# Sixteen-head attention in a four-layer kernel: head pairs in two halves of the partitions, parts staged through a DRAM scratch

## The reference

```python
# layer 0; layer 2 is the same without biases, and causal
q = (x @ Wq.T + bq).reshape(b, s, 16, 8)
k = (x @ Wk.T + bk).reshape(b, s, 16, 8)
v = (x @ Wv.T + bv).reshape(b, s, 16, 8)
w = jnp.einsum('bshd,bzhd->bhsz', q, k) / jnp.sqrt(8.0)
w = jax.nn.softmax(w, axis=-1)
vw = jnp.einsum('bhsz,bzhd->bshd', w, v).reshape(b, s, 128)
x = _layernorm(x + vw @ Wo.T + bo)
```

## Time and profile before

| | |
|---|---|
| median of 3 runs | 1496.15 us (1493.22 to 1500.85) |
| the profiled execution | 1497.72 us |
| its span in the profile | 1496.0 us |
| TensorE (PE) matmul busy | 1135.4 us (76%) |
| VectorE (DVE) busy | 952.6 us (64%) |
| ScalarE (ACT) busy | 614.8 us (41%) |
| GpSimd (POOL) busy | 486.2 us (32%) |
| mean granted TensorE clock | 0.846 of full speed |
| bytes moved by DMA | 117.02 MB, 152567 packets |

### The profile page before, as it was taken

One profiled execution on the slowest core, in us unless ns is written; L12 is line 12 of the kernel. 1 busy time (PEld: TensorE's weight loads), 2 busy tenths in 40 slices (PEclk: granted clock), 3 DMA queues, 4 the chain that ended last, 5 costly groups with the idle time before them and its releaser, 6 DMA issues.

```text
span 1496.0 us, 32177 instructions
## 1 busy us (share of the span) xinstructions
PE 1135.4 (76%) x9171; PEld 822.8 (55%) x9171; DVE 952.6 (64%) x3478; ACT 614.8 (41%) x1352; POOL 486.2 (32%) x695
## 2 busy tenths in 40 slices
PE   2799899889199994776728998999976899337950
PEld 1355555554188883664516776777654566225730
DVE  3688888886423324996836776777557687761237
ACT  1266556656044441335403554555554232113410
POOL 6112433434535453233441111111024111352553
PEclk9599889989599996997657999999977797558985
DMA  4655445531367767211025443444010000133523
GB/s 118 72 59 62 70 67 76 69 59 40 115 196 201 207 198 228 74 43 32 18 31 70 53 53 48 52 55 47 17 29 28 22 25 11 44 110 92 167 78 91
DMA packets 152567, 117.02 MB, mean 78 GB/s; under 512 B 16001, under 2 KB 140674, under 8 KB 152322
## 3 DMA queue, kind: packets, MB, share of 16 engines
q1 hardware_dynamic: 145282, 101.18, 34.2%
q0 software_dynamic: 7168, 14.37, 2.9%
HBM read 47.26 MB, written 23.41 MB: 47 GB/s over the span
## 4 chain that ended last, share of the span: by engine, by line
PE 46%; DVE 23%; issue 10%; DMA 7%; POOL 6%; SPq 3%; ACT 3%; DVEq 1%; POOLq 0%; ACTq 0%
PE po L1485 7%; PE po L431 6%; DVE xg L334 4%; PE pt L1479 4%; DVE mx L601 4%; PE pm L1479 3%; SPq L367 3%; PE pt L391 2%; PE pt L394 2%; PE pm L412 2%; DMA xs<-xg 2%; POOL rstd L327 2%; PE pm L417 2%; PE pm L418 2%; PE p L522 2%
## 5 line engine op out<-in xcount | busy, mean ns | idle before, releaser
L601 DVE TENSOR_REDUCE mx<-pm 128x2 f32<-128x512 f32 (+1 forms) x512 | 306.3, 619 | 163.2 <-PE pm L418 97.8
L553 ACT ACTIVATE ex<-pt 128x512 f32<-128x512 f32 (+1 forms) x512 | 271.1, 544 | 207.9 <-PE pt L391 99.3
L324 POOL TENSOR_SCALAR ve<-mv 128x2 f32<-128x2 f32 x96 | 25.5, 266 | 560.6 <-DVE mv L318 560.6
L1562 POOL DMA_INDIRECT result<-ye,to_row x128 | 122.9, 960 | 151.3 <-issue 107.2
L431 PE MATMUL po<-ex,va 128*32 128x256 f32 (+1 forms) x2048 | 157.7, 381 | 5.2 <-ACT ob L562 5.2
L412 PE MATMUL pm<-ks,qs 96*128 96x256 bf16 x512 | 110.7, 303 | 11.5 <-DVE mx L601 10.9
L308 ACT COPY xt<-p 128x256 f32<-128x256 f32 x112 | 41.8, 373 | 175.1 <-PE p L304 175.1
L1485 PE MATMUL po<-he,we 128*128 128x256 f32 (+1 forms) x448 | 112.9, 395 | 0.6 <-DVE yt L1523 0.4
L334 DVE TENSOR_SCALAR xg<-res,mv,rstd 128x128 f32<-128x128 f32 (+1 forms) x192 | 90.1, 536 | 32.6 <-POOL rstd L327 32.6
L391 PE MATMUL pt<-qs,ks 99*128 99x256 bf16 x512 | 105.7, 292 | 6.4 <-DMA qs<-mt 3.1
L303 PE MATMUL p<-ident,xs 128*128 128x128 f32 x112 | 40.4, 361 | 85.2 <-DMA xs<-xg 81.9
(11 more groups left out here) (281 smaller groups left out, 2788.5 us busy)
## 6 DMA issues: line engine op xcount, KB each, us to landing
we<-in_pack SPq DMA_DIRECT2D x40, 514.5 KB
xs<-xg SPq DMA_DIRECT2D x112, 128.0 KB, 2.2
qs<-parts SPq DMA_DIRECT2D x192, 64.0 KB
ks<-parts SPq DMA_DIRECT2D x192, 64.0 KB
we<-in_pack SPq DMA_DIRECT2D x16, 512.0 KB
xe<-sorted SPq DMA_DIRECT2D x56, 132.0 KB, 2.2
yr<-result SPq DMA_DIRECT2D x48, 128.0 KB, 2.2
xr<-xg SPq DMA_DIRECT2D x32, 128.0 KB, 4.8
```

Of the source, the lines that this page charges most:

```text
L553: nc.scalar.activation(ex[j % 2][:, 2 * u:2 * u + 2, lo:S], pt[:, u, :].rearrange("p (b k) -> p b k", k=S)[:, :, lo:S], ACT.Exp).then_inc( ...
L601: nc.vector.tensor_reduce(mx[q.slot % 2][:, qt, 4 * b + 2 * u:4 * b + 2 * u + 2], pm[:, u, :].rearrange("p (b k) -> p b k", k=S)[:, :, 0:h ...
L1562: pool.indirect_dma_start(out=rows, out_offset=bass.IndirectOffsetOnAxis(ap=to_row[q.slot][0:m, i:i + 1], axis=0), in_=ye[q.slot][0:m, i, ...
```

## The change

Heads 2h and 2h+1 form a pair. The even head of each pair sits in partitions 0 to 47 of the stacks and the odd one in partitions 64 to 111; the maxima follow in rows 48 to 50 and 112 to 114. Each stack is now 128 partitions by 8 pairs by 256 tokens. For every (j, u) one function `scores` issues what `scores_m` and `scores_t` issued, alternating between the two: for u = 0 `scores_m` works on the even heads and `scores_t` on the odd ones, for u = 1 the other way round, so that two neighbouring matmuls read different halves of the partitions and write different PSUM banks. All waits of both are ahead of the first matmul. The causal mask also fits in 64 rows: an identity half times a mask half, twice (256 and 128 columns, each for both heads), in place of two products of 128 columns.

Parts go to the stacks in two hops: six DMAs write them (in the order of the six products) to a DRAM scratch `scr`, SP waits until all six have landed, and four DMAs of 48 partitions read them back, one per stack and half. The zeroing of the stacks on POOL and its semaphore are gone; DVE sets rows 32 to 63 and 96 to 127 of `ks` to one at the start. Two transposes of 48 rows replace one of 96 for the maxima; `mt` is 48 by 256. POOL makes the mask and identity halves with 12 affine selects where it made two.

```diff
-        STACK, MAX_AT = 48, 96
-        ks = [sb(f"ks{i}", [MAX_AT + 3, HEADS, S], BF16) for i in range(SLOTS)]
+        STACK, HALF, HP = 48, P // 2, HEADS // 2
+        ks = [sb(f"ks{i}", [P, HP, S], BF16) for i in range(SLOTS)]
...
+        scr = nc.dram_tensor("scr", (SLOTS, 2, PRODUCTS, P, S), BF16).ap()
...
-                    for t in range(2):
-                        sp.dma_start(qs[q.slot][MAX_AT:MAX_AT + 3, :, t * P:t * P + P],
-                                     mt[q.slot % 2][STACK * t:STACK * t + STACK, :]).then_inc(mrows[q.slot], 16)
+                    for of_pair in range(2):
+                        r = HALF * of_pair + STACK
+                        sp.dma_start(qs[q.slot][r:r + 3, :, :],
+                                     mt[q.slot % 2][3 * HP * of_pair:3 * HP * (of_pair + 1), :]).then_inc(mrows[q.slot], 16)
                 if (q := at(1)):
                     wait_apart(sp, parts_pool, 2 * (a + q.n + 1), passed)
+                    if a == 0:
+                        sp.wait_ge(consts_v, CONSTS_V)
+
+                    s = q.slot % 2
+                    for c, n_c in ((0, 3), (3, 2), (5, 1)):
+                        sp.dma_start(scr[q.slot, 0, c:c + n_c].rearrange("c p k -> p c k"), parts[s][:, 0:n_c, 0, :]
+                                     ).then_inc(to_scr, 16)
+                        sp.dma_start(scr[q.slot, 1, c:c + n_c].rearrange("c p k -> p c k"),
+                                     parts[s][:, 3 - n_c:4 - n_c, 1, :].to_broadcast([P, n_c, S])).then_inc(to_scr, 16)
+                    wait_apart(sp, to_scr, 16 * PRODUCTS * (a + q.n + 1), passed)
+
                     wait_apart(sp, ts_ps, 16 * (a + q.back(3)), passed)
-                    sp.wait_ge(stack_zero, SLOTS * (2 if a == 0 else 3))
-
-                    for r, of in enumerate(PAIRS):
-                        for i, stack in enumerate((qs, ks)):
-                            sp.dma_start(stack[q.slot][r * DH:r * DH + DH, :, :].rearrange("r h k -> r (h k)"),
-                                         parts[q.slot % 2][:, of[i], i, :]).then_inc(stacked[q.slot], 16)
+                    for i, stack in enumerate((qs, ks)):
+                        src = scr[q.slot, i].rearrange("c (d h g) k -> (c d) h g k", h=HP, g=2)
+                        for of_pair in range(2):
+                            r = HALF * of_pair
+                            sp.dma_start(stack[q.slot][r:r + STACK, :, :], src[:, :, of_pair, :]
+                                         ).then_inc(stacked[q.slot], 16)
...
+            def scores(qt, jt, qm, jm, u):
...
+                gm, gt = u, 1 - u
+                mine, theirs = pm[:, u, :], pt[:, u, :]
...
+                for e in range(2):
+                    if qm:
+                        keys = half(ks, qm, gm, STACK, 2 * bm + e)
+                        queries = half(qs, qm, gm, STACK, 2 * bm + e)[:, qtile * P:qtile * P + P]
+                        k0, k1 = (qtile * P, qtile * P + P) if causal else (0, S)
+                        last_m = pe.matmul(mine[:, e * S + k0:e * S + k1], queries, keys[:, k0:k1],
+                                           start=not causal, stop=e == 1 or not causal)
+                    if qt:
+                        keys = half(ks, qt, gt, STACK + 3, 2 * bt + e)[:, ktile * P:ktile * P + P]
+                        queries = half(qs, qt, gt, STACK + 3, 2 * bt + e)
+                        k0, k1 = (ktile * P, ktile * P + P) if causal else (0, S)
+                        last_t = pe.matmul(theirs[:, e * S + k0:e * S + k1], keys, queries[:, k0:k1],
+                                           start=not causal, stop=e == 1 or not causal)
...
-            for i in range(SLOTS):
-                stacks = (qs, ks) if a == 0 else (qs,)
-                for stack in stacks:
-                    nc.gpsimd.memset(stack[i][0:MAX_AT, :, :].rearrange("p h k -> p (h k)").bitcast(F32),
-                                     0.0).then_inc(stack_zero, 1)
```

More of the change, by code:

```diff
@@ L197, in post_norm_stack @@
         with ExitStack() as mem:
-            qs = [sb(f"qs{i}", [MAX_AT + 3, HEADS, S], BF16, mem) for i in range(SLOTS)]
+            qs = [sb(f"qs{i}", [P, HP, S], BF16, mem) for i in range(SLOTS)]
             ex = [sb(f"ex{i}", [P, 4, S], F32, mem) for i in range(2)]
@@ L266, in post_norm_stack @@
         FIRST = 2
-        CONSTS = 11
+        CONSTS = 21
         cleared = sem("cleared")
@@ L377, in heads_tensor @@
         def heads_tensor(pe, a, g, causal, layer, routed):
-            def scores_t(q, j, u):
-                b, kt = j // 2, j % 2
-                pe.wait_ge(stacked[q.slot], SPLITS * (a // SLOTS + q.turn + 1))
-                pe.wait_ge(mrows[q.slot], 32 * (a // SLOTS + q.turn + 1))
-                wait(pe, e_sb, 16 * (a + q.n) + 2 * j + u - 1)
-                for i in (2 * u, 2 * u + 1):
-                    h = 4 * b + i
-                    dst = pt[:, i // 2, (i % 2) * S:(i % 2) * S + S]
-                    lhs = ks[q.slot][:, h, kt * P:kt * P + P]
-                    rhs = qs[q.slot][:, h, :]
-                    if not causal:
-                        last = pe.matmul(dst, lhs, rhs, start=True, stop=True)
-                        continue
-                    d0 = kt * P
-                    pe.matmul(dst[:, d0:d0 + P], ident16[:, :], hide_k[:, :], start=True, stop=False)
-                    last = pe.matmul(dst[:, d0:d0 + P], lhs, rhs[:, d0:d0 + P], start=False, stop=True)
-                    if kt == 0:
-                        last = pe.matmul(dst[:, P:S], lhs, rhs[:, P:S], start=True, stop=True)
-                last.then_inc(ts_ps, 1)
@@ L400, in scores_m, with half @@
-            def scores_m(q, j, u):
-                b, qt = j // 2, j % 2
-                if j == 0:
-                    pe.wait_ge(stacked[q.slot], SPLITS * (a // SLOTS + q.turn + 1))
-                wait(pe, ms_max, 16 * (a + q.n) + 2 * j + u - 1)
-                for i in (2 * u, 2 * u + 1):
-                    h = 4 * b + i
-                    dst = pm[:, i // 2, (i % 2) * S:(i % 2) * S + S]
-                    lhs = qs[q.slot][0:MAX_AT, h, qt * P:qt * P + P]
-                    rhs = ks[q.slot][0:MAX_AT, h, :]
-                    if not causal:
-                        last = pe.matmul(dst, lhs, rhs, start=True, stop=True)
-                        continue
-                    d0 = qt * P
-                    if qt == 1:
-                        pe.matmul(dst[:, 0:P], lhs, rhs[:, 0:P], start=True, stop=True)
-                    pe.matmul(dst[:, d0:d0 + P], ident16[:, :], hide_q[:, :], start=True, stop=False)
-                    last = pe.matmul(dst[:, d0:d0 + P], lhs, rhs[:, d0:d0 + P], start=False, stop=True)
-                last.then_inc(ms_ps, 1)
+            def half(stack, q, g, k, at_head):
+                return stack[q.slot][HALF * g:HALF * g + k, at_head, :]
@@ L464, in between @@
                     wait_apart(pe, m_parts, 4 * (a + q.n + 1), passed)
-                    pe.transpose(p0[0:96, S:2 * S].bitcast(BF16)[:, 0:P],
-                                 mp[q.slot % 2][:, :, :, :].rearrange("p t c h -> p (t c h)"),
-                                 ident16[:, :]).then_inc(mt_ps, 1)
+                    for t in range(2):
+                        last = pe.transpose(p0[0:STACK, S:2 * S].bitcast(BF16)[:, t * P:t * P + P],
+                                            mp[q.slot % 2][:, t, :, :, :].rearrange("p g c h -> p (g c h)"),
+                                            ident16[:, :])
+                    last.then_inc(mt_ps, 1)
                 if (j, u) == (2, 0) and (q := at(1)):
@@ L1708, in _ @@
                 nc.vector.memset(xt[i][:, 0:1], 0.0).then_inc(consts_v, 1)
-                nc.vector.memset(ks[i][MAX_AT:MAX_AT + 3, :, :].rearrange("p h k -> p (h k)").bitcast(F32),
-                                 float(np.uint32(0x3F803F80).view(np.float32))).then_inc(consts_v, 1)
+                for g in range(2):
+                    nc.vector.memset(ks[i][HALF * g + 32:HALF * g + HALF, :, :].rearrange("p h k -> p (h k)").bitcast(F32),
+                                     float(np.uint32(0x3F803F80).view(np.float32))).then_inc(consts_v, 1)
             dve.wait_ge(w_in, W_IN)
@@ L1738, in _ @@
             g = nc.gpsimd
-            for t, v in ((ident, 0.0), (ones, 1.0), (upto, 1.0), (hide_k, 0.0), (hide_q, 0.0), (half, -0.5),
-                         (zt, 0.0), (zero_col, 0.0), (ones16, 1.0), (upto16, 1.0), (ident16, 0.0)):
+            for t, v in ((ident, 0.0), (ones, 1.0), (upto, 1.0), (hide_k, 0.0), (hide_q, HIDE), (half, -0.5),
+                         (zt, 0.0), (zero_col, 0.0), (half_id, 0.0), (ones16, 1.0), (upto16, 1.0), (ident16, 0.0)):
                 g.memset(t[tuple([slice(None)] * len(t.shape))], v).then_inc(cleared, 1)
-            CLEARED = 11
+            CLEARED = 12
             pool.wait_ge(cleared, CLEARED)
```

97 lines of the change are left out of this document (72 added, 25 removed).

## The result

The changed kernel takes 1491.9 us (median of 20 runs, 1487.6 to 1497.2) against 1498.8 us for the kernel before beside it: a ratio of 0.9961, 95% interval 0.9943 to 0.9979. That is 0.4% faster, inside the half per cent that I had called no change, and 42 us above my forecast. The profiled execution took 1494.6 us with a span of 1492.9.

What follows compares the result with a forecast made beforehand. PE was taken to bound the causal stage, PE and DVE together the first. From the profiled execution, 1497.7 - 24 - 10 - 9 - 4 = 1450.7, so 1450 us; range 1422 to 1502, held 8 in 10.

Steps and rivals of the forecast that it cites:

- no change: Whole kernel: a difference within about 0.5% (7.5 us), which a measurement can't tell apart; chance 0.10.
- Score blocks: Causal score products: pairs overlap fully, blocks take 0.41 us (j even) and 0.29 (j odd), -3.8 us per step.
- The rivals in which pairs run in turn: Score products: no overlap; 1498 us without loss at form changes (chance 0.10), 1534 us with PE drained at each (0.12).
- Changes of form and W: PE's causal step: tiling changes cost 0.25 us each, +2.0 us; PE's own work W goes from 17.6 to 15.8 us.
- Transfers: Stacking through scratch: writes land at 5.8 us, the chain to scores_t takes about 15 us instead of 16.4.
- the near end: Stacking: the faster transfer case, with reads into 48 partitions at the pace of `yr` and `out_x`, 256 and 249 GB/s.
- Causal stage, -24 us: Causal stage: the step falls to 16.2 us, 2.0 us less in each of 12 steps.
- the gain stays in PE: Rival: waits for DVE and ACT; causal steps win 1.0 us, first-stage steps nothing; 1473 us, chance 0.20.
- First stage, -10 us: First stage: overlap shortens PE's blocks at the lower clock; 20.1 us per step instead of 21.1, over 10 steps.
- Filling, -9 us: Start of both stages: the third load of x lands 11.4 to 12 us after stacking starts, instead of 16.3.
- Zeroing, -4 us: Causal stage's start: without POOL's zeroing, q and k start at about 758.1 us instead of 762.66.

Runs made afterwards that it cites:

- b_scr: The kernel before with the new transfers through DRAM scratch alone, stacks in the old layout; 1479.7 us, ratio 0.9897.
- a_light: The changed kernel with DVE's maxima taken over only the first 32 keys of a row; 1456.9 us, ratio 0.9704.
- hybrid: The kernel before with new transfers in both stages, and halves and pairs in the causal stage only; 1473.7 us, ratio 0.9821.
- b_scr48: b_scr with stacks of 48 + 3 rows, no zero rows or zeroing, products one kind after the other; 2081.6 us, ratio 1.3865.
- a_serial: The changed kernel with both kinds of a visit's score products in the same half of the rows; 1816.9 us, ratio 1.2107.
- a_twice: The changed kernel with all four score products of each first-stage block issued twice; 1489.8 us, ratio 0.9967.
- b_scr_m48: b_scr with the pm products on 48 of their 96 rows, pt products kept at 99; 1913.5 us, ratio 1.2712.
- b_light: The kernel before with DVE's maxima taken over only the first 32 keys of a row; 1488.1 us, ratio 0.9919.
- a_dup1: The changed kernel with the first pair of score products of each first-stage block issued twice; 1484.4 us, ratio 0.9937.
- a_turn_first: The changed kernel with first-stage pt products waited for and issued first, then pm; causal stage still paired; 1485.7 us, ratio 0.9933.
- a_turn: The changed kernel with pt and pm products issued one kind after the other in both stages, behind the same joint waits; 1518.4 us, ratio 1.0101.

## Why the prediction was wrong, step by step

The spans of the two profiled executions, 1496.0 and 1492.9 us, differ by these parts: up to the first `ob` -7.3, from there to the last `ob` of the first stage +16.4, on to the first of the causal stage -8.2, on to its last -3.1, and the rest -0.9. Against the forecast of -10 and -24 the two stages miss by 26 us (8.1 of them behind the twelfth `ob`) and 21 us, and these two make up the error.

- **Score blocks.** Right: full overlap, 0.40 and 0.29 us. The rivals in which pairs run in turn fell.
- **Changes of form and W.** Right in sum: PE is busy for 15.7 us of a causal step, against a forecast W of 15.8. Four transposes at 0.11 us each leave 0.24 us of the 0.68 above for the changes on both sides, where I charged 0.25.
- **Transfers.** The chain was right (5.95 us for the writes, no wait of `scores_t` for DMAs), and the 48-row reads took the near end. Its effect on the causal step was wrong: I charged 0.6 us per step to the wait in the earlier trace rows, and b_scr, which has it no more, keeps 18.1 us.
- **Causal stage, -24 us.** This term was mis-sized. I let the step follow W, 16.2 us. PE won its 1.8 us and then stood for 1.9 us at lumps of DVE and ACT work, 7.1 us at `mx` in 90. The step won 0.7 us, a little less than the 1.0 of my rival "the gain stays in PE"; a_light shows that `mx` is 0.6 us of it, and the wait for ACT comes next.
- **First stage, -10 us.** This is the step that failed. It said that of the 3.2 us at the lower clock "overlapping halves them, -1.8 us", and so took the clock as given while the products changed. (The 3.2 us were read off one stretch; by the 0.90 of the earlier trace rows it was 4.2 a step.) Measured, the time at 1.2 GHz grew from 4.2 to 8.8 us a step, and halves and pairs cost 21 us there (hybrid). The rival had "nothing" for this stage, and tied the clock to a PE that idles. Idling is not what sets the kernels apart: with PE idle for 14 to 17 of 160 us those with 96 and 99 rows are granted 0.90 to 0.95, those with half-row products 0.79 to 0.86, and b_scr48 and a_serial are granted 0.50 through long stretches without a gap. That the lower clock carries the loss is shown by a_twice in mid stage only (0.95, and most steps shorter in spite of 3.6 us more work); the kernel as a whole was no faster. In the changed kernel pairs fill both halves in the score blocks, and it holds 1.00 in the causal stage but 0.80 in the first; why it is 0.80 there and not higher stays open.
- **Filling, -9 us.** Right in kind: 7.3 us in the first stage (first `ob` at 76.7 instead of 84.1), and 5.0 us off the wait in the causal one, of which the path from the first `qk` to the first `ob` keeps 3.2 (63.3 to 60.0 us).
- **Zeroing, -4 us.** Right. From the last `ob` of the first stage to the first `qk` of the causal one it is 388.9 us before and 384.0 now, 4.9 less; the rows of the forecast themselves gave 5.35 - 0.60 = 4.75. The four kernels that zero a second time (before, b_scr, b_scr_m48, b_light) need 388.9 to 392.9 us, the other ten 383.1 to 386.1, and the slow DVE instruction, alone 5.28 us, stands in those four and in none of the others. No run takes the zeroing out by itself.
- **The tails.** I had no term for them. From the twelfth `ob` to the last, the first stage's end takes 71.9 us instead of 63.8, at a clock of 0.81 from 310 to 370 us instead of 0.96. In the causal stage's end it varies where the code is one and the same: from the twelfth `ob` to the last 63.0 us at a clock of 0.86 in the changed kernel and in a_twice, 57.5 at 1.00 in a_dup1, a_turn_first and hybrid. These 5.5 us are most of what the profiles of a_dup1 and a_turn_first are ahead of the changed kernel's; I have one profile of each and can't say how often either end comes.

The range held 1491.9, but the point was 42 us low, and no change had 0.10. That it was inside owes more to the range's width than to a rival that came true. Nearly all that I said of PE's work came true, and little of it reached the end.

## What to carry to other kernels

Before products are moved into parts of the array's rows, ask what will keep the granted clock up: read PEclk for each stretch beside PE's busy time, since a PE that is 100% busy at 0.50 looks like a bound and is a loss. A stage bound by two engines in lumps returns only a part of what one of them wins; shorten the other's lumps in a trial (as a_light) to see what is there to be had. And where a change has separable parts, try them apart: here one part alone gave more than twice the whole.

## What the runs showed of the hardware that I had not expected

- PE was granted 0.50 for whole stages without idling (160.00 of 160 us busy in b_scr48, 92.00 of 92 in a_serial), with products of 48 and 51 rows that all or mostly run alone; with 96 and 99 rows, in the same order, b_scr has 0.94 from 140 to 300 us.
- With about the same idle time of PE from 140 to 300 us (14 to 17 us) kernels with 96 and 99 rows were granted 0.90 to 0.95 and kernels with half-row products, most of them side by side, 0.79 to 0.86.
- Repeating half-row products to no use raised it again, from 0.80 to 0.86 and 0.95 (a_dup1, a_twice).
- Products issued in blocks of one kind and then the other ran side by side all the same where their halves differed (a_turn: 950.78 beside 950.77, three places ahead of its turn).
- Writing the parts to DRAM and reading them back into 48 rows was quicker for what waits on it than crowding 8 rows from SBUF: x came 11.3 us after the first issue, not 16.3, though the bytes go twice (142 MB in all instead of 117): 104 and 103 GB/s over the stretches of the earlier trace rows instead of 71 and 52.
